# A gated graph network on one core: eight of the candidate's rounded passes, instead of four, between w4's rounded and low passes

## The chip, the cores and the metric

The kernel runs on one core of a Trainium2 chip. The metric is the device time of one execution in microseconds (us), lower is better; where several runs are shown, their median counts. The page and the trace describe one profiled execution.

## The reference, cut to what matters

There are two layers. The first is an attention over 64 nodes for each of 128 graphs; it is not touched by the change. The second is a gated graph network with three steps. `x` is (128, 64, 256), `adj` is (64, 64) and serves as both matrices, so `a_in` and `a_out` are the same product.

```python
h = relu(layernorm(x))
x = x + attention(h, adj, Wq, Wk, Wv)
h = relu(layernorm(x))
for _ in range(3):
    a = adj @ h                                    # for each graph
    av = concatenate([a, a])
    z = sigmoid(av @ w3.T + b3 + h @ u3.T + bu3)
    r = sigmoid(av @ w4.T + b4 + h @ u3.T + bu3)
    hv = tanh(av @ w5.T + b5 + (r * h) @ u5.T + bu5)
    h = (1 - z) * h + z * hv
return x + h
```

## The kernel before

**Tiles.** Eight graphs (512 tokens) make a group; there are 16 groups, worked on in 8 pairs. A state tile has the features on partitions, as two halves (C = 2) of 128 x 512. Two state buffers, s = 0 and 1, hold the two groups of a pair, and all work alternates between them.

**Passes.** A matrix product in near-float32 precision is made of three passes in the type fp32r: each operand is split into a rounded part (`_hi`, ScalarE) and the rest (`_lo`, VectorE), and TensorE adds `W_hi*x_hi`, `W_lo*x_hi` and `W_hi*x_lo`. One pass is one matmul of 128x128 by 128x512. The text calls the passes on `a_hi` *rounded* passes (`rounded_a`: 4 for each output half o, two input halves by W_hi and W_lo) and those on `a_lo` *low* passes (`low_a`: 2 for each output half).

**Windows.** One step of the network for one group is a window. There are 48, numbered w = 6i + k: round i works on one pair, k = 0 to 5 says which window of the round it is. k = 2 and 4 also carry attention products of the next pair, k = 3 and 5 its weighted sums, k = 0 and 5 turn the start states of the next groups. On TensorE a window is a fixed list:

1. `reset_gate_h`: 12 passes of u3 on h into `gate`, used by both r and z
2. `gate_and_candidate_a`: the products with a. w4 goes into `gate` (which then holds the argument of r), w5 into `cand`
3. `update_gate`: 12 passes of wz = w3 - w4 on a into `gate`, which turn r's argument into z's; wz[o] waits for `r_ready`, that is until ScalarE's sigmoid r_s[o] has read `gate`
4. in k = 2 and 4 the products of queries (`fea<-hxT_hi`, `fea<-hxT_lo`), values and scores
5. `candidate_rh`: 12 passes of u5 on rh = r * h into `cand`, behind `rh_hi_ready` and `rh_lo_ready`
6. `adjacency`: adj times the *other* group's state, into `fea`, from `t_s` (k = 1 to 4) or h0 (k = 0 and 5)

**Who waits for whom.** `r_full` is raised by the last low pass of w4 for each half. ScalarE then computes r_s (line 870), VectorE rh (line 1222), ScalarE rh_hi, VectorE rh_lo. `fea_taken` says that VectorE has made `a_lo` out of `fea`. `c_ready` says that ScalarE's tanh of the previous window has read `cand`.

Every engine works through its own list in order. ScalarE's list in window k = 1 is r_s, rh_hi, four instructions `hx` (the normalised input of the next attention), z_s, t_s, c_s (tanh), a_hi. t_s is the other group's new state in token order: it has gone from VectorE's transpose `h_turned` through SyncE's store to a scratch tensor and four loads into `h_back`. In k = 4 and 0 four instructions `h_blk` stand ahead of r_s on ScalarE. VectorE's list in window k = 0 is the update of the other group's state (with `h_turned` and a_lo), `final`, rh, rh_lo, the transposes `h<-h_back` of the next start state (they wait for four loads), its h_lo, d_s; in k = 1 it is the update, `final`, statistics of the input, rh, rh_lo and so on. In k = 2 and 4 two transposes `hxT<-hx_back`, which wait for loads too, stand ahead of rh, and hxT_lo behind it. POOL copies h0 in order (line 389, four copies, in k = 4 and 0) and keeps the residual (line 400). SyncE issues all transfers in order; in k = 0 (`turn_h0_and_state`) it stores h_blk, waits for `h_turned` and stores it (line 285), waits for the first store, and issues the four loads of h0 (line 252).

Of the kernel before, what the change touches and what calls it, by code (L numbers as in the profile page):

```python
# [32 lines left out]
def gated_graph_kernel(nc, x, adj, adj_t, wq, wk, wv_t, w3_t, b3, u3_t, bu3, w4_t, b4, w5_t, b5,  # L33
# [8 lines left out]
    C = D // P  # L42
# [33 lines left out]
    with ctx:  # L76
# [3 lines left out]
        def sem(name):  # L80
            return ctx.enter_context(nc.semaphore(name))
# [76 lines left out]
        cand = ctx.enter_context(nc.psum_tensor("cand", [P, C, T], f32))  # L158
# [35 lines left out]
        r_ready, z_ready, c_ready = sem("r_ready"), sem("z_ready"), sem("c_ready")  # L194
# [234 lines left out]
        def _(pe):  # L429
# [7 lines left out]
            def one(dst, lhs, rhs, start=False, stop=False):  # L437
                return nc.tensor.matmul(dst, lhs, rhs, start=start, stop=stop, skip_group_check=True)  # L438

            def weight(n, c, o):  # L440
                return W_hi[n][:, c, o * P:(o + 1) * P], W_lo[n][:, c, o * P:(o + 1) * P]
# [176 lines left out]
            def rounded_a(dst, n, s, o, start=False):  # L618
                for c in range(C):
                    w_hi, w_lo = weight(n, c, o)  # L620
                    one(dst[:, o, :], w_hi, a_hi[s][:, c, :], start=start and c == 0)
                    one(dst[:, o, :], w_lo, a_hi[s][:, c, :])

            def low_a(dst, n, s, o, stop=False):
                for c in range(C):
                    last = one(dst[:, o, :], weight(n, c, o)[0], a_lo[s][:, c, :], stop=stop and c == C - 1)
                return last

            def gate_and_candidate_a(w, s, n_a, c_first=None):
                pe.wait_ge(a_hi_ready, 2 * w + 2)  # L630
                for o in range(C):
                    rounded_a(gate, "w4", s, o)
                if c_first is not None:
                    pe.wait_ge(*c_first)
                if isinstance(w, int) and w == 0:
                    pe.wait_ge(w_lo_ready, 6)
                else:
                    pe.wait_ge(c_ready, 2 * w - 1)
                rounded_a(cand, "w5", s, 0, start=True)
                pe.wait_ge(fea_taken, 2 * n_a + 2)  # L640
                for o in range(C):
                    low_a(gate, "w4", s, o, stop=True).then_inc(r_full, 1)
                low_a(cand, "w5", s, 0)
                if not (isinstance(w, int) and w == 0):
                    pe.wait_ge(c_ready, 2 * w)
                rounded_a(cand, "w5", s, 1, start=True)
                low_a(cand, "w5", s, 1)

            def update_gate(w, s):

# [32 lines left out]
            def window(i, k, use, attention=True, new=True):  # L683
# [9 lines left out]
                else:  # L693
                    pe.wait_ge(h_lo_ready, 8 * i + 2 * (k - 1))
                reset_gate_h(w, s)
                gate_and_candidate_a(w, s, use("adj %d" % (k - 1)) if k > 1 else
                                     use_in_round("adj 0" if k else "adj 5", i - 1))
                update_gate(w, s)
# [56 lines left out]
            weighted_sum_start(1, n("sum 1"))  # L755
            pe.wait_ge(w_lo_ready, 5)
            gate_and_candidate_a(0, 0, n("adj first"), (h_new_ready, C))
            update_gate(0, 0)
            tok_done(n("sum 1"))
# [674 lines left out]
```

## Time and profile before

| | |
|---|---|
| median of 3 runs | 877.17 us (875.93 to 878.3) |
| the profiled execution, its own time | 877.4 us |
| its span, from the first to the last instruction | 875.6 us |
| mean granted clock of TensorE | 0.997 |
| TensorE busy | 862.2 us, 98% |
| VectorE busy | 743.3 us, 85% |
| ScalarE busy | 491.0 us, 56% |
| POOL busy | 117.1 us, 13% |

Engines in the rows: PE is TensorE's matmul, PEld its weight load, DVE VectorE, ACT ScalarE, POOL GpSimd, SP or SPq SyncE. A row of the timeline gives the start in us from the start of the span, the duration, engine, line and operation, the written and read tiles, the shape and how many instructions were merged into it; the bracket is the idle time of the engine before it and what ended that. The ends of matmuls are modelled: they overlap, and the distance of two starts is what a matmul costs. An instruction that waits for nothing is recorded as starting some 0.08 us ahead of the recorded end of the one before it on VectorE. For r_s, rh, rh_lo and so on there are two instructions to a window, one for each half; they mostly stand in one row.

### The profile page before, as it was taken

The page shows a single profiled execution, that of the slowest core. Times are in us where ns is not written, and L with a number is a line of the kernel's source. Part 1 is how long each engine was busy: PE and PEld are TensorE (multiplying, and loading weights), DVE is VectorE, ACT ScalarE, POOL GpSimd, SP SyncE. Part 2 cuts the span into 40 slices and gives each one's busy share as a digit, 9 for nine tenths or more (in the row PEclk, how much of TensorE's full clock was granted, in tenths as well). Part 3 has the DMA queues.
Part 4 walks back from the last instruction along what each step waited for, and adds up shares of the span by engine and source line. Part 5 has one row for each costly group of instructions (what it writes and reads, how often), then busy time and mean ns, then how long its engine had stood idle before and what let it go on. Part 6 is the DMA issues. An engine that isn't in the chain of part 4 may idle for free.

```text
span 875.6 us, 19328 instructions
## 1 busy us (share of the span) xinstructions
PE 862.2 (98%) x7356; PEld 709.4 (81%) x7356; DVE 743.3 (85%) x1518; ACT 491.0 (56%) x881; POOL 117.1 (13%) x161
## 2 busy tenths in 40 slices
PE   8999999999999999999999999999999999999997
PEld 7878888888888888888888888888888787888886
DVE  5888889888898888888989889898889888898676
ACT  5456654646556464655645656456555556545553
POOL 1110112201131010210102101120011301121000
PEclk9999999999999999999999999999999999999999
DMA  6014232533245232541424514155231543234222
GB/s 188 2 49 145 91 104 96 172 119 97 97 131 182 73 121 98 165 150 60 141 87 145 178 52 143 63 168 169 73 121 66 170 150 97 98 106 136 74 73 97
DMA packets 88452, 99.53 MB, mean 114 GB/s; under 512 B 8641, under 2 KB 80577, under 8 KB 88385
## 3 DMA queue, kind: packets, MB, share of 16 engines
q1 hardware_dynamic: 88384, 98.50, 35.3%
q8 instruction: 58, 0.95, 0.5%
q14 instruction: 10, 0.07, 0.0%
HBM read 50.76 MB, written 47.71 MB: 112 GB/s over the span
## 4 chain that ended last, share of the span: by engine, by line
PE 84%; DVE 5%; ACT 4%; issue 4%; DMA 2%; POOL 1%; SPq 1%; DVEq 0%; ACTq 0%; POOLq 0%
PE cand L438 26%; PE gate L438 13%; PE gate L433 9%; PE gate L434 9%; PE gate L435 9%; PE fea L590 6%; PE fea L523 2%; PE tok L433 2%; PE tok L434 2%; PE tok L435 2%; PE fea L433 2%; PE fea L435 1%; PE fea L434 1%; PE tok L566 1%; DMA h_back<-h_trip 1%
## 5 line engine op out<-in xcount | busy, mean ns | idle before, releaser
L870 ACT ACTIVATE r_s<-gate,b_r 128x512 f32<-128x512 f32 x96 | 60.7, 684 | 122.2 <-PE gate L438 122.2
L776 ACT ACTIVATE h_hi<-h 128x512 fp32r<-128x512 f32 x92 | 57.0, 630 | 67.8 <-DVE h L996 48.8
L1222 DVE TENSOR_TENSOR rh<-r_s,h 128x512 f32<-128x512 f32 x96 | 64.9, 715 | 22.8 <-ACT r_s L870 22.3
L378 POOL TENSOR_TENSOR rstd<-vare,minus_half 128x4 f32<-128x4 f32 x32 | 41.6, 1301 | 293.2 <-DVE vare L1030 293.2
L433 PE MATMUL gate<-h_hi,W_hi_u 128*128 128x512 f32 x192 | 80.1, 417 | 0.2 <-DVE h_lo L996 0.2
L433 PE MATMUL gate<-a_hi,W_hi_wz 128*128 128x512 f32 x192 | 74.8, 390 | 0.6 <-DVE W_lo_wz L996 0.6
L434 PE MATMUL gate<-h_lo,W_hi_u 128*128 128x512 f32 x192 | 75.2, 392 | 0.0
L438 PE MATMUL cand<-rh_hi,W_hi_u 128*128 128x512 f32 x188 | 75.0, 399 | 0.1
L435 PE MATMUL gate<-h_hi,W_lo_u 128*128 128x512 f32 x192 | 75.1, 391 | 0.0
L438 PE MATMUL cand<-a_hi,W_lo_w 128*128 128x512 f32 x192 | 74.7, 389 | 0.0
L438 PE MATMUL gate<-a_hi,W_lo_w 128*128 128x512 f32 x192 | 74.7, 389 | 0.0
L435 PE MATMUL gate<-a_hi,W_lo_wz 128*128 128x512 f32 x192 | 74.7, 389 | 0.0
L438 PE MATMUL gate<-a_hi,W_hi_w 128*128 128x512 f32 x192 | 74.7, 389 | 0.0
L434 PE MATMUL gate<-a_lo,W_hi_wz 128*128 128x512 f32 x192 | 74.7, 389 | 0.0
L438 PE MATMUL cand<-a_hi,W_hi_w 128*128 128x512 f32 x192 | 74.7, 389 | 0.0
L776 ACT ACTIVATE rh_hi<-rh 128x512 fp32r<-128x512 f32 x96 | 58.5, 632 | 28.6 <-DVE rh L1222 28.6
L438 PE MATMUL cand<-rh_hi,W_lo_u 128*128 128x512 f32 x188 | 73.3, 390 | 0.0
L883 ACT ACTIVATE z_s<-gate,b_z 128x512 f32<-128x512 f32 x96 | 63.0, 680 | 16.7 <-PE gate L435 16.5
L1207 DVE STREAM_TRANSPOSE h_turned<-h 128x512 f32<-128x512 f32 x94 | 66.4, 706 | 5.6
L1190 DVE TENSOR_TENSOR c_s<-z_s,c_s 128x512 f32<-128x512 f32 x94 | 62.8, 668 | 9.1 <-ACT c_s L896 9.1
L996 DVE TENSOR_TENSOR h<-c_s,d_s 128x512 f32<-128x512 f32 (+1 forms) x98 | 66.8, 681 | 3.4
L1185 DVE SCALAR_TENSOR_TENSOR d_s<-z_s,h 128x512 f32<-128x512 f32 x96 | 62.1, 683 | 8.0 <-ACT z_s L883 8.0
(160 smaller groups left out, 2024.3 us busy)
## 6 DMA issues: line engine op xcount, KB each, us to landing
h_back<-h_trip SPq DMA_DIRECT2D x216, 128.0 KB, 2.8
h_trip<-h_turned SPq DMA_DIRECT2D x40, 512.0 KB, 2.6
x_s<-x SPq DMA_DIRECT2D x15, 512.0 KB, 5.2
out<-o_s SPq DMA_DIRECT2D x15, 512.0 KB, 3.7
hx_back<-hx_trip SPq DMA_DIRECT2D x56, 128.0 KB, 2.8
h_trip<-h_blk SPq DMA_DIRECT2D x14, 512.0 KB, 3.1
hx_trip<-hx SPq DMA_DIRECT2D x14, 256.0 KB, 3.3
hx_trip<-hx SPq DMA_DIRECT2D x28, 128.0 KB, 3.2
```

The lines of the kernel that those rows point to most:

```text
L433: nc.tensor.matmul(dst, l_hi, r_hi, start=start, stop=False, skip_group_check=True)
L434: nc.tensor.matmul(dst, l_hi, r_lo, start=False, stop=False, skip_group_check=True)
L435: return nc.tensor.matmul(dst, l_lo, r_hi, start=False, stop=stop, skip_group_check=True)
L438: return nc.tensor.matmul(dst, lhs, rhs, start=start, stop=stop, skip_group_check=True)
L776: return nc.scalar.activation(dst, src, ACT.Copy)
L870: nc.scalar.activation(r_s[:, c, :], gate[:, c, :], ACT.Sigmoid, bias=b_r[:, c:c + 1]).then_inc(r_ready, 1)
L883: nc.scalar.activation(z_s[:, c, :], gate[:, c, :], ACT.Sigmoid, bias=b_z[:, c:c + 1]).then_inc(z_ready, 1)
L996: return nc.vector.tensor_tensor(dst, a, b, ALU.subtract)
L1185: nc.vector.scalar_tensor_tensor(d_s[:, c, :], z_s[:, c, :], 1.0, h[s][:, c, :], ALU.subtract, ALU.mult).then_inc(diff_ready, 1)
L1190: nc.vector.tensor_tensor(c_s[:, c, :], z_s[:, c, :], c_s[:, c, :], ALU.mult).then_inc(prod_ready, 1)
L1207: nc.vector.transpose(h_turned[:, :, :, c, :].rearrange("p a q f -> p q a f"), h[o][:, c, :]).then_inc(h_is_turned, 1)
L1222: nc.vector.tensor_tensor(rh[:, c, :], r_s[:, c, :], h[s][:, c, :], ALU.mult).then_inc(rh_ready, 1)
```

## The change

In `gate_and_candidate_a` all eight rounded passes of the candidate are issued behind w4's rounded passes; before, it was the four of `cand[0]`. The low passes of w4, which raise `r_full`, come behind them, and the candidate's four low passes come last, together. The wait on `c_ready` for `cand[1]` moves with its passes. In window 0 there is no such wait.

```diff
                 else:
                     pe.wait_ge(c_ready, 2 * w - 1)
                 rounded_a(cand, "w5", s, 0, start=True)
+                if not (isinstance(w, int) and w == 0):
+                    pe.wait_ge(c_ready, 2 * w)
+                rounded_a(cand, "w5", s, 1, start=True)
                 pe.wait_ge(fea_taken, 2 * n_a + 2)
                 for o in range(C):
                     low_a(gate, "w4", s, o, stop=True).then_inc(r_full, 1)
-                low_a(cand, "w5", s, 0)
-                if not (isinstance(w, int) and w == 0):
-                    pe.wait_ge(c_ready, 2 * w)
-                rounded_a(cand, "w5", s, 1, start=True)
-                low_a(cand, "w5", s, 1)
+                for o in range(C):
+                    low_a(cand, "w5", s, o)
```

## Rows read from the trace of the kernel before

**Rows 1.** The page, part 1: busy us, share of the span, instructions of each engine

```profile
PE 862.2 (98%) x7356; PEld 709.4 (81%) x7356; DVE 743.3 (85%) x1518; ACT 491.0 (56%) x881; POOL 117.1 (13%) x161
```

**Rows 2.** Waits of TensorE, whole span: us in total, times, longest us

```profile
PE fea L590 <- ACT t_s L776: 1.9, 4, 0.7
```

**Rows 3.** Timeline of TensorE in window 24 (k = 0)

```profile
468.63 1.07 PE L438 MATMUL gate<-a_lo,W_hi_w 128*128 128x512 f32 x4
...
471.35 0.39 PE L433 MATMUL gate<-a_hi,W_hi_wz 128*128 128x512 f32 x1
...
474.07 0.39 PE L438 MATMUL cand<-rh_hi,W_hi_u 128*128 128x512 f32 x1
```

**Rows 4.** Timeline of SyncE, ScalarE and VectorE in window 24

```profile
467.80 0.34 SPq L285 DMA_DIRECT2D h_trip_last<-h_turned  x1
...
468.89 1.78 SPq L252 DMA_DIRECT2D h_back<-h_trip  x4
469.29 1.27 ACT L870 ACTIVATE r_s<-gate,b_r 128x512 f32<-128x512 f32 x2 [3.05 <-PE gate L438]
...
470.08 1.30 DVE L1222 TENSOR_TENSOR rh<-r_s,h 128x512 f32<-128x512 f32 x2 [1.13 <-ACT r_s L870]
...
471.48 1.95 DVE L996 TENSOR_TENSOR rh_lo<-rh,rh_hi 128x512 fp32r<-128x512 f32 x2
...
473.48 1.30 DVE L1044 STREAM_TRANSPOSE h<-h_back 128x512 f32<-128x512 f32 x2
```

**Rows 5.** Timeline of window 25 (k = 1)

```profile
484.21 1.27 ACT L870 ACTIVATE r_s<-gate,b_r 128x512 f32<-128x512 f32 x2 [2.69 <-PE gate L438]
...
485.96 1.29 DVE L1222 TENSOR_TENSOR rh<-r_s,h 128x512 f32<-128x512 f32 x2
...
486.69 1.23 ACT L776 ACTIVATE rh_hi<-rh 128x512 fp32r<-128x512 f32 x2 [1.22 <-DVE rh L1222]
...
490.95 1.14 ACT L776 ACTIVATE t_s<-h_back 128x512 f32<-128x512 f32 x2
...
491.80 1.16 PE L590 MATMUL fea<-adjT,t_s 64*64 64x64 f32 x64
```

**Rows 6.** Timeline of window 26 (k = 2)

```profile
500.39 1.30 DVE L1044 STREAM_TRANSPOSE hxT<-hx_back 128x512 f32<-128x512 f32 x2 [2.32 <-DMA hx_back<-hx_trip]
...
504.17 0.47 PE L433 MATMUL fea<-hxT_hi,W_hi_m 128*128 128x512 f32 x1
```

**Rows 7.** Timeline of window 23 (k = 5)

```profile
454.37 1.27 ACT L870 ACTIVATE r_s<-gate,b_r 128x512 f32<-128x512 f32 x2 [5.87 <-PE gate L438]
455.36 1.28 DVE L1222 TENSOR_TENSOR rh<-r_s,h 128x512 f32<-128x512 f32 x2
```

**Rows 8.** Timeline of window 13 (k = 1), ScalarE and TensorE

```profile
280.57 1.14 ACT L776 ACTIVATE t_s<-h_back 128x512 f32<-128x512 f32 x2
...
281.33 1.16 PE L590 MATMUL fea<-adjT,t_s 64*64 64x64 f32 x64 [0.26 <-ACT t_s L776]
```

**Rows 9.** Timeline of VectorE in windows 6 and 12 (k = 0)

```profile
157.58 1.30 DVE L1044 STREAM_TRANSPOSE h<-h_back 128x512 f32<-128x512 f32 x2 [0.88 <-DMA h_back<-h_trip]
...
263.11 1.30 DVE L1044 STREAM_TRANSPOSE h<-h_back 128x512 f32<-128x512 f32 x2 [0.48 <-DMA h_back<-h_trip]
```

**Rows 10.** Timeline of window 22 (k = 4)

```profile
431.01 1.09 PE L438 MATMUL gate<-a_lo,W_hi_w 128*128 128x512 f32 x4
...
432.16 1.24 ACT L870 ACTIVATE r_s<-gate,b_r 128x512 f32<-128x512 f32 x2
...
432.46 2.35 POOL L389 COPY h<-h_blk 128x256 f32<-128x256 f32 x4
...
432.86 1.69 DVE L1222 TENSOR_TENSOR rh<-r_s,h 128x512 f32<-128x512 f32 x2 [0.24 <-ACT r_s L870]
...
434.48 1.48 DVE L996 TENSOR_TENSOR hxT_lo<-hxT,hxT_hi 128x512 fp32r<-128x512 f32 x2
...
436.47 0.39 PE L433 MATMUL fea<-hxT_hi,W_hi_m 128*128 128x512 f32 x1
```

## What I predict, and how it is worked out

> **What bounds the kernel now.** I read the page first: TensorE is busy for 98% of the span, VectorE for 85% [rows 1]. The time can change only by idle time that TensorE gains or loses. Next the waits of TensorE. The only wait inside the steady loop is that of the adjacency product for `t_s`, 1.9 us in four windows [rows 2]; nothing is listed for the low passes of w4 behind the wait on `fea_taken`. So the wait that this change covers with four more matmuls costs nothing today. There is nothing to win at that place, and the question is what the change delays.
>
> The timeline of window 24 (k = 0) shows the order that is edited: from the first low pass of w4 at 468.63 to the first wz pass at 471.35 there are 4 + 2 + 4 + 2 = 12 matmuls in 2.72 us, 0.227 each without a hole [rows 3].
>
> **The change, part by part.** It adds and removes no instruction: in each of 48 windows four matmuls of `cand[1]` and one wait change their place. Their 4 x 0.227 = 0.91 us are on TensorE's path before and after: 0.
>
> *The wait on `c_ready` for `cand[1]`* moves ahead by 6 matmuls, 1.36 us; queued behind it are then the low passes of w4, and with them r_s. It asks for the tanh of the previous window, whose last product ended before the adjacency product and 24 further passes (24 x 0.227 = 5.4 us) were issued, and no wait of this kind is listed. Cost 0.
>
> *The low passes of w4* move back by 0.91 us, and with them `r_full`, for which ScalarE's r_s waits, then VectorE's rh, ScalarE's rh_hi, VectorE's rh_lo and the last products of the candidate. wz does not move. In window 24 the two r_s begin at 469.29 and end at 470.56 [rows 4], later 471.47. wz[0] at 471.35 needs only the first, which ends 0.58 before the second, then at 470.89: 0.46 to spare. wz[1] begins six matmuls after wz[0], at 472.71: 1.24 to spare. rh_lo's pair ends at 473.43, `cand<-rh_hi` begins at 474.07 and the first pass on rh_lo four matmuls later, at 474.98 [rows 3, 4]: 0.91 is hidden there too. Taken alone, each window hides the delay.
>
> But VectorE works in order, and where it had been waiting for r_s, all that is behind moves too. So I went through the kinds of window by what VectorE waited for before rh:
> - k = 1 and 3: for nothing but its own backlog. In window 25 r_s begins at 484.21, rh only at 485.96, 1.07 after the first result [rows 5]. The 0.91 of the same window is absorbed.
> - k = 2: rh stands behind the transposes of `hx_back`, which wait for a transfer, 2.32 in window 26 [rows 6]. Absorbed.
> - k = 5: in window 23 the first r_s ends at 455.06 and rh starts at 455.36 [rows 7], so 0.61 to 0.64 is passed on to window 24. There VectorE idles 1.13 for r_s [rows 4], and it is gone. On its way it moves a store on SyncE's queue (rival 2).
> - k = 0: VectorE idles until r_s and then goes on through the splits, the transposes `h<-h_back`, the update of window 25, `final` and the statistics, up to rh of window 25, with one wait that can give way (below). Here the delay travels. rh starts 0.10 after the end of its r_s, where 0.03 is usual, so I take 0.85 of the 0.91.
> - k = 4: below.
>
> *Where it arrives.* In window 25 ScalarE waits for that rh (1.22 before rh_hi at 486.69) and then works without a hole over hx and z_s to t_s at 490.95; TensorE's adjacency product starts at 491.80, 0.85 after it [rows 5]. In window 13, where TensorE did wait (0.26), that distance is 0.76 [rows 8]. So window 25 has 0.09 to spare; window 31, read alike, 0.07; windows 7, 13, 19 and 37 have none, they are the four of [rows 2]. What VectorE brings late into k = 1, TensorE loses.
>
> *What absorbs it on the way.* `h<-h_back` in k = 0 also waits for its transfer, which hangs on ScalarE's h_blk and not on r_s. VectorE idles there 0.88 in window 6 and 0.48 in window 12 [rows 9]; read alike, 0.49 in window 18 and 1.36 in window 36; in window 24 only 0.05 (473.43 to 473.48) [rows 4], in window 30 0.08. An instruction that waits for nothing starts 0.08 ahead of the recorded end of the one before, so the real waits are 0.96, 0.56, 0.57, 1.44, 0.13 and 0.16. The 0.85 fills these first. What is left: window 6: 0; 12: 0.29; 18: 0.28; 24: 0.85 - 0.13 - 0.09 = 0.63; 30: 0.85 - 0.16 - 0.07 = 0.62; 36: 0. Window 42 leads to a window without attention work and has room; in window 0 rh waits for VectorE's own weight splits. Sum 1.82. The query products of window 26, which start late already (the first takes 0.47, a cold start [rows 6]), get the 0.09 that the adjacency's margin swallowed: 1.9 us in all.
>
> *k = 4*, the tight one. In window 24 r_s starts 0.66 after the first low pass; in window 22 that pass is at 431.01 and r_s at 432.16 [rows 10], so ScalarE was 0.49 late by itself (h_blk), and r_s and rh move by 0.42. hxT_lo ends at 435.96, the query products that read it begin at 436.47: of 0.51 would be left 0.09, and about 0.10 is what a product there needs. But POOL's four copies at 432.46 are started by h_blk, which stays. rh's pair takes 1.69 and hxT_lo's 1.48 beside them, where a pair alone takes 1.29 [rows 5, 10]: 0.6 in all. With rh at 433.28 the first two copies are over, and VectorE gets at least 0.2 back. Then 0.29 is left and the price is 0. The other bound: no relief, and each of seven windows pays about 0.03 and a cold start of 0.08, 7 x 0.11 = 0.8. I take 0, as the copies' start doesn't depend on r_s.
>
> Beside this: the Trainium skill (SBUF — State Buffer, Who interferes with whom) says that a VectorE instruction with two SBUF inputs and a GpSimd instruction that reads SBUF exclude each other, the first one keeping the port to its end. By that rule a copy that is over before rh starts costs nothing, the sum's 0; without it the sum would be 0.8 higher. The trace agrees as far as it goes (1.69 beside the copies, 1.29 without).
>
> **Sum.** The profiled execution took 877.4 us, 875.6 of them span and 1.8 around it. 877.4 + 1.9 = 879.3; the median of the runs shown is 0.2 below that execution: 879.1 us, +0.2%.
>
> **The rivals.**
> 1. *All is hidden*, 877.2 us. The transfers into k = 0 land as late as in windows 6 and 36 in every round, and the 0.85 drops into that wait. For it: these waits differ widely from round to round, so the program doesn't fix them. Against it: two of six rounds are early here.
> 2. *The transfer moves too*, slower. The loads of h0 stand on SyncE behind a store of the turned state (467.80, 0.34 long) that the delay from k = 5 makes 0.61 later. It would end at 468.75, 468.79 with the step behind it; the loads leave at 468.89 [rows 4]. 0.10 decides. Beyond it, or if the later store slows the loads beside it by as much, nothing is absorbed: 6 x 0.85 - 0.16 = 4.9, 882.1 us.
> 3. *k = 4 pays as well*, slower: no relief by POOL's copies, 1.9 + 0.8 = 2.7, 879.9 us.
> 4. *Faster*: a late a_lo is covered by 0.91 more. No such wait is listed; were all of [rows 2] to vanish, it would be 875.3 us, still within the bound below. More needs something that I don't see.
>
> **How the numbers follow.** A measurement of this kernel can tell some 0.3%, 2.6 us, from no change: faster is below 874.5, slower above 879.8. Forecast 0.48, of which 0.04 lies above 879.8, since the waits for transfers vary; rival 1 0.15; rival 2 0.20; rival 3 0.12; rival 4 and the unseen 0.05. Faster 0.05, same 0.44 + 0.15 = 0.59, slower 0.04 + 0.20 + 0.12 = 0.36. Range: from 876.4 (rival 1 less 0.8, a third of the spread of the three runs, since it is a median) to 881.9, just under rival 2 at its full price, of which a part is likelier than all.
>
> **What would show it.** TensorE's step of 0.227 unchanged; r_s 0.91 later against wz in k = 0, 1, 2, 3 and 5; before rh in k = 0 VectorE idle 1.4 instead of 1.13 (0.91 more, less the 0.61 from k = 5); the idle time before `h<-h_back` gone or shorter by 0.85; TensorE's wait for `t_s` in k = 1 in six windows instead of four, 3.5 to 4 us instead of 1.9; no wait before the query products in k = 4. It is wrong if TensorE waits for r_s or rh_hi in k = 3 or 5, or if the loads of h0 in k = 0 leave later against TensorE than before.

## The result, and the profile after

| | before | after |
|---|---|---|
| median (5 runs each, on the same chip) | 876.79 us (875.93 to 878.3) | 880.68 us (879.73 to 881.74) |
| ratio, 95% interval | 1 | 1.0048 (1.0032 to 1.0063) |
| the profiled execution, its own time | 877.4 us | 880.68 us |
| its span | 875.6 us | 878.9 us |

The changed kernel is slower by 0.48%, 3.9 us. That lies in the range of the prediction (876.4 to 881.9), but past its time (879.1) and in the case "slower by over 0.3%", which had 0.36, not in the likeliest one.

TensorE's waits after, as in [rows 2] (us in total, times, longest):

```profile
PE fea L590 <- ACT t_s L776: 4.3, 6, 0.7
```

The wait named in the forecast has grown from 1.9 us in four windows to 4.3 us in six; no wait for r_s, rh_hi or `fea_taken` has come up. Timeline of window 24 (k = 0) after, SyncE, TensorE, ScalarE, POOL and VectorE, which answers to [rows 3, 4]:

```profile
470.31 0.34 SPq L285 DMA_DIRECT2D h_trip_last<-h_turned  x1
470.76 2.17 SPq L252 DMA_DIRECT2D h_back<-h_trip  x4
471.40 1.07 PE L438 MATMUL gate<-a_lo,W_hi_w 128*128 128x512 f32 x4
472.05 1.27 ACT L870 ACTIVATE r_s<-gate,b_r 128x512 f32<-128x512 f32 x2 [3.96 <-PE gate L438]
472.83 1.04 POOL L400 COPY resid<-x_s 128x1024 f32<-128x1024 f32 x1
472.84 2.18 DVE L1222 TENSOR_TENSOR rh<-r_s,h 128x512 f32<-128x512 f32 x2 [1.39 <-ACT r_s L870]
473.21 0.39 PE L433 MATMUL gate<-a_hi,W_hi_wz 128*128 128x512 f32 x1
475.12 1.29 DVE L996 TENSOR_TENSOR rh_lo<-rh,rh_hi 128x512 fp32r<-128x512 f32 x2
476.33 1.30 DVE L1044 STREAM_TRANSPOSE h<-h_back 128x512 f32<-128x512 f32 x2
```

To compare executions I measure each time from the first wz pass of the window, whose place in TensorE's list the change does not touch: 471.35 before [rows 3], 473.21 here.

| window 24, us from the first wz pass | before | after | later by |
|---|---|---|---|
| SyncE's store of `h_turned` | -3.55 | -2.90 | 0.65 |
| the first load of h0 leaves | -2.46 | -2.45 | 0.01 |
| the issue of the four loads ends | -0.68 | -0.28 | 0.40 |
| the last of them has landed | 2.10 | 2.64 | 0.54 |
| r_s starts | -2.06 | -1.16 | 0.90 |
| rh starts | -1.27 | -0.37 | 0.90 |
| rh_lo ends | 2.08 | 3.20 | 1.12 |
| `h<-h_back` starts | 2.13 | 3.12 | 0.99 |

The store, the first load, r_s and rh are where the forecast had them. Two things are not. One is the loads: only the first leaves on time. SyncE issues the four in 2.17 us instead of 1.78 [rows 4], the fourth starts at -0.71 instead of -1.12, and it lands 0.54 later. The other is VectorE: rh starts 0.90 later, but rh_lo ends 1.12 later. The reason for that stands in two rows of the fence. POOL's copy of the residual (line 400) starts at 472.83, rh at 472.84; the copy takes 1.04, and rh's pair takes 2.18, 0.89 more than its 1.29 [rows 5]. Before, the same copy began inside VectorE's rh pair and stretched to 1.51, and it was rh_lo behind it that took 1.95 instead of 1.29 [rows 4]:

```profile
470.77 1.51 POOL L400 COPY resid<-x_s 128x1024 f32<-128x1024 f32 x1
```

So the copy cost VectorE 0.66 before and 0.89 after: 0.90 + 0.88 (rh's pair, 2.18 against 1.30) - 0.66 (rh_lo's, 1.29 against 1.95) = 1.12. The Trainium skill (SBUF — State Buffer, Who interferes with whom) says that of two such instructions the first keeps the port to its end. The trace agrees here: with 0.01 of a start the copy runs undisturbed in 1.04, and rh's pair loses 0.89.

Where the 0.99 arrives, window 25 (k = 1), to be read against [rows 5]:

```profile
488.82 1.29 DVE L1222 TENSOR_TENSOR rh<-r_s,h 128x512 f32<-128x512 f32 x2
...
489.55 1.24 ACT L776 ACTIVATE rh_hi<-rh 128x512 fp32r<-128x512 f32 x2 [1.29 <-DVE rh L1222]
...
493.80 1.14 ACT L776 ACTIVATE t_s<-h_back 128x512 f32<-128x512 f32 x2
494.56 1.16 PE L590 MATMUL fea<-adjT,t_s 64*64 64x64 f32 x64 [0.70 <-ACT t_s L776]
```

The adjacency product stands 0.76 behind t_s, the distance that the forecast took for a TensorE that waits, and it waited 0.70.

**The account.** The start of `h<-h_back` after the first wz pass, in the six rounds that have a next one with attention work:

| window | 6 | 12 | 18 | 24 | 30 | 36 |
|---|---|---|---|---|---|---|
| before | 2.96 | 2.56 | 2.57 | 2.13 | 2.15 | 3.44 |
| after | 3.26 | 3.12 | 3.11 | 3.12 | 3.12 | 3.26 |
| later by | 0.30 | 0.56 | 0.54 | 0.99 | 0.97 | -0.18 |
| TensorE's loss two windows on | 0.29 | 0.56 | 0.49 | 0.89 | 0.87 | -0.20 |

The last row is the growth of the distance from window w to window w + 2 on TensorE. It is the row above it, less the margins of 0.09 and 0.07 of windows 25 and 31. Together 2.9 us. The other 0.4 of the span's 3.3 are single distances: 0.37 from window 2 to 3, 0.29 from 38 to 39, -0.38 from 26 to 27, and 0.13 from 22 to 23. The first three are windows of k = 2 whose query products begin late in one of the two executions (at 3.05 and 2.93 after the first wz pass in windows 2 and 38 after, at 2.98 in window 26 before, otherwise at 2.72), because the loads `hx_back` landed late. That differs between executions of one kernel: in e0, the changed kernel again, they begin at 2.72 in windows 2 and 38 and at 3.04 in window 26. The 0.13 is a window of k = 4, of which more below.

### The profile page after: what moved, and what is told of

Its sections match the earlier page's. It is cut to its first block, busy times and chain, and to the rows that moved or that the text cites. A ratio compares the mean times of both kernels' runs of the same rounds, so it can differ in the third digit from the quotient of the medians.

```text
span 878.9 us, 19328 instructions
## 1 busy us (share of the span) xinstructions
PE 863.0 (98%) x7356; PEld 709.1 (81%) x7356; DVE 743.0 (85%) x1518; ACT 488.4 (56%) x881; POOL 106.5 (12%) x161
## 4 chain that ended last, share of the span: by engine, by line
PE 77%; DVE 9%; ACT 6%; issue 5%; DMA 1%; POOL 1%; SPq 0%; DVEq 0%; ACTq 0%; POOLq 0%
PE cand L438 23%; PE gate L438 12%; PE gate L433 9%; PE gate L434 8%; PE gate L435 8%; PE fea L590 5%; PE fea L523 2%; PE tok L433 2%; ACT hx L799 2%; PE tok L434 2%; PE tok L435 2%; PE fea L433 2%; PE fea L435 1%; PE fea L434 1%; PE tok L566 1%
## 5 line engine op out<-in xcount | busy, mean ns | idle before, releaser
L1222 DVE TENSOR_TENSOR rh<-r_s,h 128x512 f32<-128x512 f32 x96 | 70.2, 771 | 35.9 <-ACT r_s L870 35.0
L896 ACT ACTIVATE c_s<-cand,b_c 128x512 f32<-128x512 f32 x94 | 61.6, 686 | 10.6 <-PE cand L438 9.7
```

Of the source, the lines that this page charges most:

```text
L896: nc.scalar.activation(c_s[:, c, :], cand[:, c, :], ACT.Tanh, bias=b_c[:, c:c + 1]).then_inc(c_ready, 1)
L1222: nc.vector.tensor_tensor(rh[:, c, :], r_s[:, c, :], h[s][:, c, :], ALU.mult).then_inc(rh_ready, 1)
```

## The experiments

Two theories on why `h<-h_back` is late in k = 0.

*A, VectorE's list:* the later r_s of k = 0 and the copy that now falls on rh keep VectorE busy until 3.1 to 3.2. The delay handed over from k = 5 counts only in that it moves the copy onto rh. The loads play no part. The expectations of e0 to e7 were written with this theory.

*B, the later of two:* the loads are late as well. The delay from k = 5 puts the state's store on SyncE's queue 0.65 later, right ahead of the loads of h0; the first of them leaves on time, but they run beside the store and land later. `h<-h_back` starts at the later of the two, VectorE free and loads landed, so that either alone would bring most of the loss and taking away one alone would give back little. B was written down after e0 to e7 had run; e8 to e11 test it.

The rival to both is that the time goes elsewhere (k = 4, window boundaries), and the t_s wait only shows it.

**Run e0: the changed kernel once more**, among the experiments, for the size of the effect.

> The changed kernel once more, beside the parts of it. Both theories: 3 to 4 us over the kernel before, TensorE waiting for t_s in six windows of k = 1, 4.0 to 4.6 us in all.

881.36 us, ratio 1.0042 (1.0027 to 1.0058): the loss is there again, `h<-h_back` at 3.12.

**Run e1: the new order in k = 0 alone**

```diff
+                ahead = w % 6 in (0,)
...
                 rounded_a(cand, "w5", s, 0, start=True)
+                if ahead:
+                    if not (isinstance(w, int) and w == 0):
+                        pe.wait_ge(c_ready, 2 * w)
+                    rounded_a(cand, "w5", s, 1, start=True)
+                    pe.wait_ge(fea_taken, 2 * n_a + 2)
+                    for o in range(C):
+                        low_a(gate, "w4", s, o, stop=True).then_inc(r_full, 1)
+                    for o in range(C):
+                        low_a(cand, "w5", s, o)
+                    return
```

This is the edit against the kernel before. Where `ahead` does not hold, its order follows.

> The new order in the windows of k = 0 alone. Theory A (the loss is VectorE's lateness at the end of k = 0, made of the later r_s and of where POOL's copy of the residual falls): the copy is not moved by k = 5, it starts some 0.6 us before rh, VectorE loses only about 0.3 us to it instead of 0.67, and rh_lo ends some 0.45 us later than before, not 1.1: about +0.5 us in all. Rival P (the later r_s alone counts, POOL does not): the full 0.85 is carried, +1.8 to +2 us. Rival S (anything but k = 0 makes the loss): 0.

877.4 us, 0.9996 (0.9985 to 1.0007): no loss. Window 24 of this kernel, POOL, VectorE and TensorE:

```profile
469.92 1.04 POOL L400 COPY resid<-x_s 128x1024 f32<-128x1024 f32 x1
470.55 1.55 DVE L1233 TENSOR_TENSOR rh<-r_s,h 128x512 f32<-128x512 f32 x2 [2.02 <-ACT r_s L881]
470.92 0.39 PE L433 MATMUL gate<-a_hi,W_hi_wz 128*128 128x512 f32 x1
472.20 1.30 DVE L1007 TENSOR_TENSOR rh_lo<-rh,rh_hi 128x512 fp32r<-128x512 f32 x2
473.42 1.30 DVE L1055 STREAM_TRANSPOSE h<-h_back 128x512 f32<-128x512 f32 x2
```

rh starts at -0.37, as in the changed kernel, so r_s is just as late. But window 23 hands nothing over: VectorE comes to its idle time early (2.02 instead of 1.39), POOL's copy starts 0.63 ahead of rh and not 0.01, and only what is left of it, 0.41, can fall on rh, whose pair takes 1.55. rh_lo ends at 2.58 instead of 3.20, `h<-h_back` starts at 2.50, where the six of the kernel before had a median of 2.56. So k = 0 by itself costs nothing that can be measured: the interval ends at +0.6 us. Theory A had said +0.5, which it holds too, so e1 does not decide between A and B. It does exclude that the later r_s alone makes the loss (+1.8 to +2).

**Run e2: the new order everywhere but in k = 0**

```diff
+                ahead = w % 6 in (1, 2, 3, 4, 5)
```

> The new order in all windows but those of k = 0. Theory A: r_s of k = 0 is where it was, but POOL's copies come 0.6 us later by k = 5 and stand beside rh and rh_lo: VectorE loses some 0.2 to 0.6 us more than before there, +0.3 to +1.5 us in all. Rival P: 0 within 0.3. Rival S: the whole +3.3.

881.62 us, 1.0046 (1.003 to 1.0062): the whole loss, without the late r_s of k = 0. Waits of TensorE, then VectorE in window 24 (first wz pass at 473.04):

```profile
PE fea L590 <- ACT t_s L787: 3.9, 6, 0.7
```

```profile
475.96 1.30 DVE L1055 STREAM_TRANSPOSE h<-h_back 128x512 f32<-128x512 f32 x2 [1.30 <-DMA h_back<-h_trip]
```

VectorE was free at 1.62 and idled 1.30 for the loads, until 2.92. Theory A had given this kernel +0.3 to +1.5 us, and it has lost 4. That is more than A can make, and B explains e1 and e2 together.

**Run e3: k = 5 and k = 0 alone**

```diff
+                ahead = w % 6 in (0, 5)
```

> The new order in k = 5 and k = 0 alone. Theory A: the state of the changed kernel in k = 0 is whole (rh_lo 1.1 us later), +2.7 to +3.3 us, TensorE waits for t_s in six windows of k = 1. Rival P: +1.8 to +2, like k = 0 alone. Rival S: less than half of the loss.

881.27 us, 1.0037 (1.0025 to 1.0048), waits for t_s 4.3 us in six windows and `h<-h_back` at 3.13, the same as with the full change. The new order in k = 1 to 4 has no part in it: the forecast's zeros there, k = 4 among them, hold.

**Run e8: k = 5 alone**, the sharper form of e2.

```diff
+                ahead = w % 6 in (5,)
```

> The new order in k = 5 alone. Theory B (two causes, each enough: the store of the turned state, 0.65 us later by k = 5, runs beside the loads of h0 and makes them land 0.4 to 0.5 us later; and r_s of k = 0 with POOL's copy makes VectorE 1.1 us later): r_s of k = 0 is not moved, rh_lo ends early, but the loads land at 2.8 to 3.1 us after the first wz pass of k = 0 instead of 2.1 to 2.5, so VectorE starts h<-h_back with them: +2 to +4 us, like all windows but k = 0. Theory A (k = 0's r_s and the copy alone): less than 1 us.

880.48 us, 1.0038 (1.0026 to 1.005). Window 24, SyncE, VectorE and TensorE:

```profile
468.82 0.34 SPq L285 DMA_DIRECT2D h_trip_last<-h_turned  x1
469.28 2.15 SPq L252 DMA_DIRECT2D h_back<-h_trip  x4
470.45 1.49 DVE L1233 TENSOR_TENSOR rh<-r_s,h 128x512 f32<-128x512 f32 x2 [0.48 <-ACT r_s L881]
471.73 0.39 PE L433 MATMUL gate<-a_hi,W_hi_wz 128*128 128x512 f32 x1
471.87 1.48 DVE L1007 TENSOR_TENSOR rh_lo<-rh,rh_hi 128x512 fp32r<-128x512 f32 x2
474.81 1.31 DVE L1055 STREAM_TRANSPOSE h<-h_back 128x512 f32<-128x512 f32 x2 [1.46 <-DMA h_back<-h_trip]
```

rh starts at -1.28, as before the change, and rh_lo ends early, at 1.62. The store leaves at -2.91 and the loads at -2.45, both as with the full change. The four loads are issued in 2.15 again. The transposes wait 1.46 and start at 3.08. Four matmuls that change their place once in six windows, with r_s and rh of k = 0 where they were, bring 3 us of the 4, through transfers.

**Run e4: the changed kernel with POOL's residual copy held back** until rh_lo is made. It takes the copy off rh.

```diff
+                pool.wait_ge(rh_lo_ready, 12 * i + 14)
```

> The changed kernel, with POOL's copy of the residual in k = 0 made to wait for rh_lo, so that it runs beside two transposes with one SBUF input. Theory A: rh takes 1.3 instead of 2.2 us for the pair, rh_lo ends 0.9 us earlier against wz, the wait for the loads of h0 is back in front of h<-h_back, and some 3 us of the loss are gone: 0 to +0.6 us over the kernel before. Rival P: nothing changes, +3.3.

880.73 us, 1.0028 (1.0013 to 1.0042). Window 24, VectorE, TensorE and POOL:

```profile
471.55 1.29 DVE L1223 TENSOR_TENSOR rh<-r_s,h 128x512 f32<-128x512 f32 x2 [1.39 <-ACT r_s L871]
471.91 0.39 PE L434 MATMUL gate<-a_hi,W_hi_wz 128*128 128x512 f32 x1
472.94 1.30 DVE L997 TENSOR_TENSOR rh_lo<-rh,rh_hi 128x512 fp32r<-128x512 f32 x2
474.45 1.04 POOL L400 COPY resid<-x_s 128x1024 f32<-128x1024 f32 x1
474.54 1.31 DVE L1045 STREAM_TRANSPOSE h<-h_back 128x512 f32<-128x512 f32 x2 [0.30 <-DMA h_back<-h_trip]
```

The edit is against the changed kernel and does what it should: rh's pair takes 1.29 again and rh_lo ends at 2.33 instead of 3.20. The gain that I expected, 3 us, did not come. VectorE now waits for the loads, and the transposes start at 2.63 in this round, 2.88 to 3.31 in four others and 4.76 in window 36. This miss is what turned me from A to B.

**Run e9: the changed kernel with the loads ahead of the store.** SyncE issues the loads of h0 first, the state's store behind them.

```diff
+                sp.wait_ge(h0_out, 16 * (g - 1))
+                blocks_back(h0_back, h0_trip[s], h0_in)
                 sp.wait_ge(h_is_turned, 2 * w)
                 sp.dma_start(h_trip_last, h_turned[:].rearrange("p a q c f -> p (a q c f)")).then_inc(h_out, 16)
-                sp.wait_ge(h0_out, 16 * (g - 1))
-                blocks_back(h0_back, h0_trip[s], h0_in)
```

> The changed kernel, with SyncE issuing the loads of h0 in k = 0 ahead of the store of the turned state. Theory B: the loads land about 0.5 us earlier or more, at or under 2.5 us after the first wz pass, but VectorE comes to them at 3.1 only: nothing is gained, +3 to +4 us over the kernel before. Rival L (the loads alone make the loss): 2.5 us or more are gained.

881.17 us, 1.004 (1.0026 to 1.0054). Window 24, SyncE, VectorE and TensorE:

```profile
469.65 1.73 SPq L252 DMA_DIRECT2D h_back<-h_trip  x4
471.50 0.35 SPq L287 DMA_DIRECT2D h_trip_last<-h_turned  x1
471.75 2.18 DVE L1222 TENSOR_TENSOR rh<-r_s,h 128x512 f32<-128x512 f32 x2 [1.38 <-ACT r_s L870]
472.11 0.39 PE L433 MATMUL gate<-a_hi,W_hi_wz 128*128 128x512 f32 x1
474.02 1.29 DVE L996 TENSOR_TENSOR rh_lo<-rh,rh_hi 128x512 fp32r<-128x512 f32 x2
475.23 1.30 DVE L1044 STREAM_TRANSPOSE h<-h_back 128x512 f32<-128x512 f32 x2
```

The loads are out of the way (the last has landed at 1.89 here, at 2.40 at the latest), the copy is not: rh's pair takes 2.18, VectorE is free at 3.20, and the transposes start at 3.12 as with the change alone. No gain either.

**Run e10: the changed kernel with both edits**, the one that B stands or falls with.

> The changed kernel with both causes taken away: the loads of h0 ahead of the store, and POOL's copy of the residual behind rh_lo. Theory B: VectorE comes to h<-h_back at 2.25, the loads are there, rh of k = 1 starts about 0.2 us ahead of its first wz pass instead of 0.7 behind it; TensorE waits for t_s 0.3 us at most in all: -1.5 to 0 us against the kernel before, 3.5 to 5 us under the changed one. Rival: the later r_s costs by another path as well, then 1 us or more of the loss stays.

874.79 us, 0.9961 (0.9946 to 0.9976): some 6 us below the changed kernel and 2.7 below the kernel before, measured beside it at 877.53. That is more than B's forecast of 3.5 to 5 and of 0 to 1.5. Window 24, SyncE, VectorE, TensorE and POOL:

```profile
468.30 1.73 SPq L252 DMA_DIRECT2D h_back<-h_trip  x4
470.15 0.35 SPq L287 DMA_DIRECT2D h_trip_last<-h_turned  x1
470.39 1.29 DVE L1223 TENSOR_TENSOR rh<-r_s,h 128x512 f32<-128x512 f32 x2 [1.38 <-ACT r_s L871]
470.76 0.39 PE L434 MATMUL gate<-a_hi,W_hi_wz 128*128 128x512 f32 x1
471.78 1.30 DVE L997 TENSOR_TENSOR rh_lo<-rh,rh_hi 128x512 fp32r<-128x512 f32 x2
473.00 1.30 DVE L1045 STREAM_TRANSPOSE h<-h_back 128x512 f32<-128x512 f32 x2
473.29 1.04 POOL L400 COPY resid<-x_s 128x1024 f32<-128x1024 f32 x1
```

The transposes start at 2.24, right behind rh_lo, in four of six rounds, and with the loads, at 2.33 and 2.28, in windows 6 and 36; the list of TensorE's waits has no t_s in it. e4 and e10 differ only in the order on SyncE's queue, e9 and e10 only in the copy's wait: each edit is worth some 6 us with the other, and alone it gives no gain clear of the noise (1.0028 and 1.004 against 1.0042 in e0, with overlapping intervals). That is what "the later of two" looks like.

**Runs e5 and e11: the same edits in the kernel before.** e5 holds back the copy; e11 has both.

> The same wait in the kernel before. Theory A: rh_lo ends 0.67 us earlier, but the loads of h0 already end last in every round (0.13 us at the least), so only 0.1 us in two rounds can be had, and TensorE has no wait there to lose: 0, within 0.3. Rival: VectorE's lateness is what ends last in windows 7, 13, 19 and 37, then -1.9.

e5: 876.99 us, 0.9994 (0.9985 to 1.0002): nothing, as expected. rh_lo ends at 1.42 instead of 2.08, but `h<-h_back` waits for its loads until 2.52 in the median of the six rounds (2.56 without the edit).

> The same two moves in the kernel before. Theory B: VectorE comes to h<-h_back at 1.4, the loads end last but early (1.5 to 2.1 after the first wz pass), no wait for t_s is left: -1.5 to -2.5 us, the fastest of all. Rival: what is gained there is lost where the loads of the state, now 2 us later, are read: 0.

e11: 876.62 us, 0.9989 (0.9978 to 1.0001), 0.9 us less than before and not clear of no change, where 1.5 to 2.5 us were expected. Waits of TensorE, then VectorE in window 24 (first wz pass at 468.76):

```profile
PE fea L591 <- ACT t_s L777: 0.7, 1, 0.7
```

```profile
470.62 1.30 DVE L1045 STREAM_TRANSPOSE h<-h_back 128x512 f32<-128x512 f32 x2 [0.43 <-DMA h_back<-h_trip]
```

Five of six rounds start at 1.86 to 2.29; in window 36 the loads landed late, at 3.60, and that one window makes the whole wait left. From the first wz pass of window 0 to that of window 47, e11 takes 1.50 us more than e10: 1.16 of it lies between windows 37 and 38, which is this late load, and 0.57 between 21 and 22, which I did not follow. The distance between the medians is 1.8.

**Runs e6 and e7: t_s ahead of z_s on ScalarE in k = 1**, in the changed kernel and in the one before. If the loss sat on ScalarE's chain from rh_hi to t_s, the earlier t_s would win it back; if it sits on VectorE, it comes up somewhere else.

```diff
-                if k == 3:
+                if k in (1, 3):
```

(The line decides before which instruction `take_back`, which issues t_s, is called; the call behind z_s falls away for k = 1.)

> The changed kernel with ScalarE making t_s ahead of z_s in k = 1, as it does in k = 3. Theory A (lateness reaches TensorE through t_s): the waits for t_s go, h<-h_back and rh stay as late; next in line are rh_hi at cand<-rh_hi (0.05 to 0.09 us to spare) and the query products of k = 2, so 2.5 to 3.5 us are gained, 0 to +1 us over the kernel before. Rival: t_s is only the first to show the lateness, and rh_hi or the tanh behind z_s takes its place: less than 1 us is gained.

e6: 880.55 us, 1.0034 (1.0021 to 1.0047). The 2.5 to 3.5 us that A expected did not come; the rival's "less than 1 us" did. Waits of TensorE:

```profile
PE fea L433 <- issue: 3.1, 6, 0.8
```

Of the waits for t_s only one of 0.2 is left, and the loss now stands at the query products of k = 2, 3.1 us in six windows, with `h<-h_back` at 3.12 as before. t_s was only the first to tell. The late rh of k = 1 has a second way to TensorE: rh_hi and, behind it on ScalarE's list, hx, whose store and loads (`hx_back`) the transposes `hxT<-hx_back` of k = 2 wait for, and then hxT_lo. In window 26 of e6 these transposes still wait 1.87 for their loads and start 0.31 ahead of the first wz pass (0.81 before), and the query products start 0.49 later than before.

> The same in the kernel before. Theory A: the 1.9 us of waits for t_s go, and it is the fastest so far: -1.5 to -2 us. Rival: z_s, later by 1.1 us, holds up VectorE's d_s and by it the next window: 0 or slower.

e7: 877.46 us, 0.9998 (0.9989 to 1.0007), where 1.5 to 2 us less were expected. No wait for t_s is listed, but the time is that of the kernel before. The second way is at work here too: the query products start 0.10 to 0.28 late in four windows of k = 2 (in the kernel before by 0.04 and 0.26 in two). Between the first wz passes of windows 0 and 47 its profiled execution takes 1.3 us less than that of the kernel before, which the medians do not show.

**All runs by one number.** The start of `h<-h_back` after the first wz pass, median of the six windows 6 to 36 of the profiled execution, beside the time. The kernel before was measured beside e0 to e11 again, at 877.53 to 877.62, so the ratios are to be compared and not the medians:

| | `h<-h_back` | ended last | median, us | ratio |
|---|---|---|---|---|
| before | 2.56 | loads | 876.79 | 1 |
| e7 | 2.49 | loads | 877.46 | 0.9998 |
| e5 | 2.52 | loads | 876.99 | 0.9994 |
| e1 | 2.49 | VectorE in 5, loads in 1 | 877.4 | 0.9996 |
| after | 3.12 | VectorE in 4, loads in 2 | 880.68 | 1.0048 |
| e0 | 3.12 | VectorE in 4, loads in 2 | 881.36 | 1.0042 |
| e3 | 3.13 | VectorE in 5, loads in 1 | 881.27 | 1.0037 |
| e6 | 3.12 | VectorE in 5, loads in 1 | 880.55 | 1.0034 |
| e9 | 3.12 | VectorE | 881.17 | 1.004 |
| e2 | 3.02 | loads | 881.62 | 1.0046 |
| e8 | 3.04 | loads | 880.48 | 1.0038 |
| e4 | 3.02 | loads | 880.73 | 1.0028 |
| e10 | 2.24 | VectorE in 4, loads in 2 | 874.79 | 0.9961 |
| e11 | 2.19 (window 36: 3.60) | loads | 876.62 | 0.9989 |

Whatever made it late, with the transposes near 2.5 the time is that of the kernel before, above 3.0 it is 0.3 to 0.5% more. Below 2.3 the two kernels differ (e10 and e11), so the number does not tell everything.

## Why the prediction was right or wrong

**Right, by its own signs.** The step of a pass unchanged; r_s later by 0.90 in k = 0; VectorE's idle time before rh 1.39 (forecast 1.4); 0.65 handed over from k = 5 (0.61 to 0.64); the wz passes with the same 0.47 behind r_s (0.46); no wait for r_s or rh_hi in k = 3 and 5; the wait for t_s in six windows, 4.3 us (3.5 to 4). Run e3 shows that k = 1 to 4 add nothing. One sign speaks against the forecast, that it is wrong if the loads of h0 leave later: the first does not, the third and the fourth do, by 0.4.

For k = 4 the term 0 was right in six of seven windows, and so was its reason. In window 28 (k = 4) of the changed kernel, POOL, ScalarE, VectorE and TensorE, to be read against [rows 10]:

```profile
540.05 1.43 POOL L389 COPY h<-h_blk 128x256 f32<-128x256 f32 x4
540.40 1.27 ACT L870 ACTIVATE r_s<-gate,b_r 128x512 f32<-128x512 f32 x2 [0.56 <-PE gate L438]
541.12 1.50 DVE L1222 TENSOR_TENSOR rh<-r_s,h 128x512 f32<-128x512 f32 x2 [0.92 <-ACT r_s L870]
542.55 1.28 DVE L996 TENSOR_TENSOR hxT_lo<-hxT,hxT_hi 128x512 fp32r<-128x512 f32 x2
544.28 0.39 PE L433 MATMUL fea<-hxT_hi,W_hi_m 128*128 128x512 f32 x1
```

The copies are over 0.36 after rh starts, rh's pair and hxT_lo together take 2.78 instead of 3.17, and 0.45 is left ahead of the query products (0.51 in [rows 10]). This is one of the best windows; in windows 4, 10, 16, 34 and 40, 0.35 to 0.46 is left. In window 22 itself the forecast's other bound came true. The copies start 0.43 later against TensorE than in [rows 10] (h_blk was late), rh's pair and hxT_lo take 3.15 together, 0.10 is left and the first query product takes 0.47. From there to window 23 TensorE takes 0.13 more than before.

**Wrong in size, first term: the 0.85 carried on in k = 0.** The mechanism was the forecast's, but the step "I take 0.85 of the 0.91" was too small by 0.27, for two reasons. It took off 0.06 for rh starting 0.10 behind its r_s, and that stayed: from the start of r_s to that of rh it is 0.79 before and after, so rh moved by the whole 0.90. And it counted only the start of rh, which leaves out 0.22. The forecast costed POOL's copies in k = 4 against VectorE and left out the one copy in k = 0, though its trace was there and rh_lo's 1.95 [rows 4] showed its price. Moved by 0.9, rh met it at its start: 1.12 instead of 0.85. Put 1.12 into the forecast's own sum: windows 6 to 36 give 1.12 - 0.96 = 0.16; 0.56; 0.55; 1.12 - 0.13 - 0.09 = 0.90; 1.12 - 0.16 - 0.07 = 0.89; 0; with the 0.09 of window 26, 3.1 us, and 877.4 + 3.1 = 880.5 us for an execution that took 880.68. So this term is the main thing that was mis-sized. That the sum comes out within 0.2 us is partly luck: in the trace the six rounds lost 2.9 and not 3.1, with -0.20 in window 36, and 0.4 came from windows that the forecast did not have. The small remainders are those of one execution, too: in e5 and e7, which have the order of the kernel before, the transposes of windows 24 and 30 start at 2.35 to 2.51 and not at 2.13 and 2.15. e1 adds that the collision needs both halves of the delay: with k = 0 alone the copy is mostly over before rh.

**Wrong in size, second term: the landing of the loads.** The forecast let the loads land where they had, as long as they left on time, and called the other case rival 2 ("or if the later store slows the loads beside it by as much"), at 0.20 and 882.1 us. It is half true. With 0.45 instead of 1.09 between the store and the first load, that load leaves on time and lands 0.85 later (0.88 against 0.03); the second takes 0.78 to issue instead of 0.46, so the fourth leaves 0.41 and lands 0.54 later. How much of that is the issue and how much the transfers side by side, no run takes apart; e9 and e10 show that it goes when the store stands behind the loads. In the changed kernel itself it costs little, as VectorE is later still in four of six windows, and only 0.14 earlier in windows 6 and 36; but it alone would bring most of the loss (e2, e8), and the case was given as an addition to the forecast where it is the other arm of a maximum. Alone it cost 3.0 us (e8) and 4.0 (e2, interval 2.6 to 5.4) against the kernel before, where rival 2 had 4.9. Rival 1 (all hidden) fell: the waits for the loads, 0.56 in two rounds and 0.13 and 0.16 in two more, could not hold 0.85, and 1.12 still less.

**The chances.** The forecast was some 0.7 us from the bound between "same" and "slower" and rested on a sum of six small remainders; an error of 0.27 in their common shift counts five times. The 0.04 that it gave to its own upper side was too little for that.

**Open.** In window 36 the last load of h0 lands at 3.4 to 4.7 in before, e2, e4, e5, e7, e8 and e11 and at 2.1 to 3.2 in the changed kernel, e0, e1, e3, e6, e9 and e10; the runs don't say why. For e11 this accounts for most of the distance to e10 in the profiled executions. Why the median of e7 gains nothing, though its waits for t_s are gone and its profiled execution is shorter, is not settled.

## What to carry to other kernels

When a delay travels through an engine that works in order, write down for each instruction behind it the later of two times, the engine free and its data there, and move *both* before you say what absorbs the delay: here two arms lay 0.1 apart, and no fix of one showed anything clear of the noise until the other was fixed too (e4 and e9: nothing clear; e10: 6 us). List also what other engines start in the idle time that shifts, above all GpSimd copies that VectorE has to sit out. And look one stage upstream: the cause in e8 is a store that a queue issues 0.65 us later, right ahead of the loads that matter. For several transfers in a row, look at the last one's issue and not only at the first one's.

## What the runs showed of the hardware that was not expected

**A copy with a start of 0.01 us.** POOL's copy of 128x1024 costs VectorE 0.89 if it starts 0.01 ahead of rh (after), 0.66 if it comes in between VectorE's instructions and stretches to 1.51 itself (before), some 0.26 if it starts 0.63 ahead (e1: 1.55 against 1.29), and nothing if it is held back (e4, e10).

**Transfers beside each other.** With the state's store issued 0.45 instead of 1.09 ahead of the four loads, the four took 2.15 to 2.17 us to issue instead of 1.78 (window 24 of e8 and the changed kernel against [rows 4]), and `h<-h_back` had to wait for them until 2.85 to 3.51 (e2, e8, five rounds each, without window 36) instead of 2.37 to 2.60 (e5, likewise). With the store behind them the issue took 1.73 (window 24 of e9 and e10), and they were there by 2.31 (e10, all six rounds; e11, but for window 36).

**The start of an execution is not fixed.** The first wz pass of window 0, TensorE, in the kernel before and in e5:

```profile
46.94 0.50 PE L433 MATMUL gate<-a_hi,W_hi_wz 128*128 128x512 f32 x1 [0.60 <-DVE W_lo_wz L996]
```

```profile
45.11 0.50 PE L434 MATMUL gate<-a_hi,W_hi_wz 128*128 128x512 f32 x1 [0.62 <-DVE W_lo_wz L997]
```

Before the first window nothing in the order of the work differs between before and e5, and it comes 1.8 us apart. In the changed kernel it lies at 46.91, so the two spans above can be compared; in e10 at 47.16. The span of one profiled execution is not a measure for an effect of 2 us unless this is taken off.
